# Second layer of a two-layer graph kernel: plain mask matmuls replaced by one Strassen level

## The chip, the cores and the metric

The kernel runs on one core of one Trainium2 chip. The metric is the device time of one execution in microseconds (us). The kernel before takes 930.55 us, the median of 3 runs (930.43 to 931.55). One profiled execution took 931.85 us; its recorded span, from the first to the last recorded instruction, is 929.8 us.

## The reference

There are N = 4096 nodes with 256 features. `adj` is a 4096 x 4096 matrix of zeros and ones. The first layer is a masked softmax over cosine similarities, the second a mean over neighbours followed by three small matrices. Cut to what matters:

```
Wh = x @ W.T;  sim = Wh @ Wh.T / (norms * norms.T + 1e-8)
mask = (adj > 0) | eye
x1 = layernorm(x + softmax(where(mask, sim, -inf)) @ Wh)

deg = sum(adj > 0, axis=1)
agg = (adj > 0) @ x1 / max(deg, 1)
out = relu(concat(x1 @ W_self + b_self, agg @ W_nb + b_nb) @ W_comb + b_comb)
y = layernorm(x1 + out)
```

The change is about the two lines that begin `deg` and `agg`, and about what feeds them and what they feed.

## The kernel before

The nodes are 32 blocks of 128, in 8 groups of four blocks (GB = 4, GW = 512). All work is written out by hand for five instruction queues; semaphores order them, and each engine runs its list strictly in the written order.

**First layer** (about 64 to 632 us). For a in 0..7 and b > a, `pair(a, b)` makes eight 128 x 512 tiles of exponentials: TensorE multiplies the unit vectors (L1027 to L1029, three fp16 products for fp32-like precision) or turns tiles it has (L1093), ScalarE takes exp (L541), VectorE applies the adjacency (L751, L776), ScalarE and VectorE split the tile into an fp16 head and tail (L548, L783), and TensorE adds up the attention (L1099 to L1101). The scores of a tile are issued three tiles ahead of its attention (AHEAD = 3), which is all the lead that VectorE has. ScalarE also writes each mask tile as fp8 ones and zeros, and SP stores it to HBM (`mask_spill`). When the row of groups a is done, VectorE takes it out of PSUM (`attention_out`, L801) and does the layer norm in pieces (`norm_work`: softmax_scale, residual, moments, normalised, split_x1), which are dealt one by one between the tiles of the next row (the list `between`). For the last two groups there is nothing left to deal them between.

**Second layer** (632 to 930 us). For each target group `aggregate` takes the 2 MB mask of the group from HBM into `mgroup` (two slots) and, for each of its four blocks and each of the 32 source blocks, loads the 128 x 128 fp8 mask as weights and streams x1 of the source, as an fp16 head with a column of ones (257 columns, L1199, the ones give the degree) and as an fp16 tail (256 columns, L1200). The first group runs over the source groups 0 to 5, then 6, then 7, so that it can start before x1 of the last groups is there. A finished block is scaled by 1/degree on ScalarE (L607), transposed on TensorE together with x1 of the block (`turn`, L1233 and L1235), split in head and tail (ScalarE L610, VectorE L940), multiplied with the combined weights (`dense`, 12 matmuls, L1245 to L1247), and finished on VectorE (`block_out`: L946, L950, L952, L953; `finish`: L959) with 1/std from GpSimd (L480, L482). `turn` and `dense` of a block are put inside the matmuls of the next block (`spread`), 6 and 18 source blocks after its start:

```
work = [lambda part=part, block=block: part(*block) for block in blocks for part in (turn, dense)]
return {6 + n * (NB - 8) // len(work): piece for n, piece in enumerate(work)}
```

so that ScalarE and VectorE have several us for each step while TensorE goes on. PSUM banks: four for the aggregation, two for `turn`, two for `dense`.

## Time and profile before

| | us |
|---|---|
| median of 3 runs | 930.55 |
| the profiled execution | 931.85 |
| its span | 929.8 |
| TensorE busy (matmuls) | 900.3 |
| VectorE busy | 608.8 |
| ScalarE busy | 412.5 |
| GpSimd busy | 65.2 |
| first matmul of the second layer, from the start | 632.09 |
| matmuls L1199 and L1200, busy together (2048) | 459.0 |

A matmul's busy time is longer than its place in the stream: neighbouring matmuls overlap, and their starts are about 0.11 us apart for 256 columns. So the counts times the distance of the starts give TensorE's time, not the sums of busy time. The span is cut in stretches by the windows view; the granted clock there is a share of TensorE's full 2.4 GHz, and 0.50 is the lower level, 1.2 GHz.

### The profile page before, as it was taken

The page shows a single profiled execution, that of the slowest core. Times are in us where ns is not written, and L with a number is a line of the kernel's source. Part 1 is how long each engine was busy: PE and PEld are TensorE (multiplying, and loading weights), DVE is VectorE, ACT ScalarE, POOL GpSimd, SP SyncE. Part 2 cuts the span into 40 slices and gives each one's busy share as a digit, 9 for nine tenths or more (in the row PEclk, how much of TensorE's full clock was granted, in tenths as well). Part 3 has the DMA queues.
Part 4 walks back from the last instruction along what each step waited for, and adds up shares of the span by engine and source line. Part 5 has one row for each costly group of instructions (what it writes and reads, how often), then busy time and mean ns, then how long its engine had stood idle before and what let it go on. Part 6 is the DMA issues. An engine that isn't in the chain of part 4 may idle for free.

```text
span 929.8 us, 21704 instructions
## 1 busy us (share of the span) xinstructions
PE 900.3 (97%) x7279; PEld 726.2 (78%) x7279; DVE 608.8 (65%) x1286; ACT 412.5 (44%) x701; POOL 65.2 (7%) x175
## 2 busy tenths in 40 slices
PE   7989999999999999999999999989899999999996
PEld 6867777777777777777777777768778888888885
DVE  2787786888766886688778788898543333333333
ACT  4955665666656565656656555550111011111110
POOL 2300000000000000000000000002110000000000
...
GB/s 257 73 150 169 147 147 157 136 171 148 157 148 154 175 153 164 138 192 143 168 178 151 165 255 151 180 117 129 70 130 41 119 125 27 120 124 23 124 28 17
DMA packets 113346, 126.03 MB, mean 136 GB/s; under 512 B 39105, under 2 KB 90594, under 8 KB 112130
## 3 DMA queue, kind: packets, MB, share of 16 engines
...
q8 instruction: 33, 0.54, 0.2%
...
## 4 chain that ended last, share of the span: by engine, by line
issue 87%; PE 5%; POOL 5%; DVE 1%; POOLq 1%; DMA 0%; ACT 0%; SPq 0%; DVEq 0%
PE ps L995 3%; POOL rstd L482 3%; POOL var_eps L480 1%; PE ps L1007 1%; DMA feat_lo<-xT 0%; PE ps L1050 0%; PE ps L1077 0%; POOLq L481 0%; DVE work L640 0%; POOLq L479 0%; DVE work L751 0%; ACT prob_hi L548 0%; DVE big L632 0%; DVE mix_extremes L709 0%; POOLq L484 0%
## 5 line engine op out<-in xcount | busy, mean ns | idle before, releaser
L1099 PE MATMUL ps<-feat_hi,prob_hi 128*128 128x257 f16 (+1 forms) x1024 | 280.0, 273 | 0.5
L1101 PE MATMUL ps<-feat_hi,prob_lo 128*128 128x257 f16 (+1 forms) x1024 | 279.6, 273 | 0.0
L1100 PE MATMUL ps<-feat_lo,prob_hi 128*128 128x256 f16 (+1 forms) x1024 | 278.9, 272 | 0.0
L1199 PE MATMUL ps<-big,mgroup 128*128 128x257 f16 x1024 | 229.5, 274 | 1.9 <-DVE big L839 1.9
L1200 PE MATMUL ps<-big,mgroup 128*128 128x256 f16 x1024 | 229.5, 274 | 0.0
L783 DVE SCALAR_TENSOR_TENSOR prob_lo<-work,prob_hi 128x512 f16<-128x512 f32 x256 | 175.8, 687 | 74.8 <-ACT prob_hi L548 72.3
L548 ACT ACTIVATE prob_hi<-work 128x512 f16<-128x512 f32 x256 | 154.6, 625 | 102.7 <-DVE work L776 48.7
L541 ACT ACTIVATE work<-ps 128x512 f32<-128x512 f32 (+2 forms) x144 | 79.3, 555 | 131.9 <-PE ps L1029 114.4
L553 ACT ACTIVATE mask<-work 128x1024 fp8e4<-128x1024 f32 x128 | 133.5, 1043 | 0.0
L1100 PEld LDWEIGHTS ps<-feat_lo,prob_hi 128*128 128x128 f16 x1024 | 100.3, 98 | 25.2
L1099 PEld LDWEIGHTS ps<-feat_hi,prob_hi 128*128 128x128 f16 x1024 | 100.0, 98 | 25.5 <-DVE prob_lo L783 1.5
L1199 PEld LDWEIGHTS ps<-big,mgroup 128*128 128x128 fp8e4 x1024 | 100.6, 98 | 14.8 <-DVE big L839 2.2
L1027 PE MATMUL ps<-unitT_lo,unitT_hi 128*128 128x512 f16 (+3 forms) x288 | 103.9, 362 | 6.9 <-DVE work L766 2.6
L1200 PEld LDWEIGHTS ps<-big,mgroup 128*128 128x128 fp8e4 x1024 | 100.6, 98 | 11.8
L1101 PEld LDWEIGHTS ps<-feat_hi,prob_lo 128*128 128x128 f16 x1024 | 100.0, 98 | 12.7
L607 ACT ACTIVATE agg_rows<-ps,rdeg 128x256 f32<-128x256 f32 x32 | 15.1, 473 | 212.7 <-DVE rdeg L935 212.7
L1028 PE MATMUL ps<-unitT_hi 128*128 128x512 f16 (+3 forms) x288 | 103.7, 361 | 0.0
L1029 PE MATMUL ps<-unitT_hi,unitT_lo 128*128 128x512 f16 (+3 forms) x288 | 103.7, 361 | 0.0
L751 DVE SCALAR_TENSOR_TENSOR work<-adj_sb,work 128x512 f32<-128x512 int32 x112 | 77.2, 689 | 27.8 <-ACT work L541 25.4
L776 DVE SCALAR_TENSOR_TENSOR work<-adj_sb,ps 128x512 f32<-128x512 int32 x112 | 76.2, 680 | 0.0
L1093 PE MATMUL ps<-ident,work 128*128 128x128 f32 x448 | 67.5, 273 | 1.5 <-DVE work L751 1.4
L480 POOL TENSOR_TENSOR var_eps<-meanvar,ln_eps 128x1 f32<-128x1 f32 x64 | 13.0, 203 | 796.3 <-DVE meanvar L824 552.4
...
## 6 DMA issues: line engine op xcount, KB each, us to landing
adj_sb<-adjT SPq DMA_DIRECT2D x128, 512.0 KB, 3.9
mask_spill<-mask SPq DMA_DIRECT2D x128, 128.0 KB, 2.7
mgroup<-mask_spill SPq DMA_DIRECT2D x8, 2048.0 KB, 8.3
...
```

The costliest lines, as they stand in the source:

```text
L541: act.activation(expo[:, r, first:], score_ps(r)[:, first:], ACT.Exp, scale=1.0 / (UNIT_SCALE * UNIT_SCALE)).then_inc(exp_ready, 1)
L548: act.activation(prob_hi[:, s, :], prob[:, s, :], ACT.Copy, scale=PROB_SCALE).then_inc(prob_hi_ready, 1)
L553: act.activation(mask[:, u_slot, :], prob[:, s:s + 2, :].rearrange("p r i -> p (r i)"), ACT.Sign, saturate=False).then_inc(mask_ready, 1)
L783: dve.scalar_tensor_tensor(out=prob_lo[:, s, :], in0=prob[:, s, :], scalar=PROB_SCALE, in1=prob_hi[:, s, :], op0=ALU.mult, op1=ALU.subtrac ...
L1027: pe.matmul(to, unitT_hi[:, k, src], unitT_lo[:, k, tgt], start=(k == 0), stop=False)
L1028: pe.matmul(to, unitT_hi[:, k, src], unitT_hi[:, k, tgt], start=False, stop=False)
L1029: ins = pe.matmul(to, unitT_lo[:, k, src], unitT_hi[:, k, tgt], start=False, stop=(k == KD - 1))
L1099: pe.matmul(acc(D + 1), prob_hi[:, s, cols], feat_hi[:, jb, 0:D + 1], start=start, stop=False)
L1100: pe.matmul(acc(D), prob_hi[:, s, cols], feat_lo[:, jb, :], start=False, stop=False)
L1101: return pe.matmul(acc(D + 1), prob_lo[:, s, cols], feat_hi[:, jb, 0:D + 1], start=False, stop=stop)
L1199: pe.matmul(agg_ps(q, D + 1), lhsT, x1_hi_of(jb // GB)[:, jb % GB, 0:D + 1], start=(jb == 0), stop=False)
L1200: ins = pe.matmul(agg_ps(q, D), lhsT, x1_lo_of(jb // GB)[:, jb % GB, :], start=False, stop=(jb == NB - 1))
```

## The change

The product mask @ x1 is cut in 2 x 2 pieces three ways: two target groups at a time (a "chunk", four of them), source groups in pairs (p = 0..3, an even and an odd group), and the 256 features in two halves. One Strassen level turns the eight piece products of a chunk and pair into seven.

- **Operands.** Masks no longer are the weights: the weights are 128 x 128 pieces of x1, as fp16 head and tail, and the mask moves, 512 columns at a time (L1474, L1475). A chunk is seven products of 32 matmuls each. Each product needs one mask operand: n11 and n22 (masks negated by the sign bit) and five differences d1, d2, d5, d6, d7. fp8 ones and zeros are bytes, so VectorE makes them by xor, as 16-bit words, 4096 words per partition and operand (`negate`, `difference`), d1 with 32-bit words (`difference_d1`).
- **Sources.** For each pair seven fp16 source pieces, five of them sums or differences of x1 halves: GpSimd adds (`sources`), VectorE splits (`source`) and copies the two plain ones (`plain_sources`). They lie where the unit vectors and features of the first layer were.
- **Degrees.** The ones column is gone. VectorE adds up mask bytes as 16-bit words over the source blocks (`degrees`, nine instructions for a target group) and TensorE sums the partitions (`degree_sums`).
- **Layer norm of x1.** The normalising and the head move from VectorE to GpSimd (`normalised`).
- **Output of a chunk.** The results come transposed, so agg needs no turn: ScalarE copies three of the products out (`keep`), GpSimd and VectorE add them up (`kept_sums`, `sums_12`, `sums_21`, `sum_of`), ScalarE and VectorE split (`agg_head`, `agg_tail`). x1 is stored to HBM as head and tail and comes back turned by DMA (`load_x1T`, four 256 KB transposes ahead of the second layer, two per group after that). `dense` has its self and neighbour part in two halves of one bank, two banks in turn, and `block_out` scales the neighbour part by 1/degree.
- **Masks from HBM** come as four 1 MB pieces per chunk, issued when all products of the chunk before last are done. Those of chunk 0 are loaded after a = 2, and its degrees, negations and d1 stand in `between` of a = 3.

```diff
+QUAD = NB // 2 * GW
+X1_SCALE = 1024.0
+SUM_SCALE = 0.5
+PRODUCTS = (("n11", 0, 0), ("n22", 1, 1), ("d1", 2, 2), ("d5", 3, 6), ("d2", 4, 5), ("d6", 0, 3), ("d7", 2, 4))
+NPROD = len(PRODUCTS)
+OPERAND_COUNT = {"n11": 1, "n22": 2, "d1": 3, "d5": 4, "d7": 5, "d2": 6, "d6": 7}
...
+            def load_raw(c, name):
+                to = unit_of(c, name).rearrange("p (r n) -> p r n", r=NPAIR)
+                ig, odd = {"n11": (2 * c, 0), "d7": (2 * c, 1), "d6": (2 * c + 1, 0), "n22": (2 * c + 1, 1)}[name]
+                sync.dma_start(to, mask_spill[ig].rearrange("p (r two b) i -> p two r (b i)", two=2, b=GB)[:, odd]).then_inc(raw_loaded[name][c % 2], 16)
...
+            def store_x1(a):
+                sync.wait_ge(x1_ready, (a + 1) * GB)
+                wait(sync, x1_stored, 16 * a)
+                wait(sync, x1h_stored, 16 * 2 * a)
+                sync.dma_start(x1_spill[a], x1_rows_of(a)).then_inc(x1_stored, 16)
+                for h, of in enumerate((x1_hi_of(a), x1_lo_of(a))):
+                    sync.dma_start(x1h_dram[h, a].rearrange("(q p) d -> p q d", p=P), of).then_inc(x1h_stored, 16)
...
+            store_x1(G - 2)
+            sync.wait_ge(attn_done, G * NB)
+            load_x1T(0)
+            load_x1T(1)
+            store_x1(G - 1)
+            sync.wait_ge(source_ready, NPAIR * NSRC)
+            sync.wait_ge(x1h_stored, 16 * 2 * G)
+            load_raw(1, "d7")
...
+            for c in range(1, NCHUNK):
+                sync.wait_ge(prod_done, NPROD * c)
+                if c + 1 < NCHUNK:
+                    for name in raw_loaded:
+                        load_raw(c + 1, name)
+                finish(2 * c - 2)
+                finish(2 * c - 1)
...
+            def normalised(a, q):
+                inv_std(a * GB + q, q)
+                if q == 0 and a % 2:
+                    wait(pool, x1_stored, 16 * (a - 1))
+                elif q == 0:
+                    pool.wait_ge(attn_done, tiles_before(a + 1)[0])
+                pool.wait_ge(rstd_ready, a * GB + q + 1)
+                to = x1_rows_of(a)[:, q, :]
+                steps.join(steps.step(pool.tensor_scalar(to, summed[:, q, 0:D], meanvar[:, q, 0:1],
+                                                         rstd[:, q:q + 1], ALU.subtract, ALU.mult)))
+                pool.tensor_scalar(x1_hi_of(a)[:, q, :], to, X1_SCALE, None, ALU.mult).then_inc(rows_hi_ready, 1)
...
+            def degrees(c, group, unit):
+                names = (("n11", "d7"), ("d6", "n22"))[1 - group]
+                total, quarter = words(unit[:, 0:QUAD // 2]), (words(unit[:, QUAD // 2:3 * QUAD // 4]), words(unit[:, 3 * QUAD // 4:]))
+                half, n = QUAD // 4, QUAD // 8
+                for name, part_sum in zip(names, quarter):
+                    dve.wait_ge(raw_loaded[name][c % 2], 16 * (c // 2 + 1))
+                    of = words(unit_of(c, name))
+                    chain.join(chain.step(dve.tensor_tensor(total, of[:, 0:half], of[:, half:], ALU.add)))
+                    chain.join(chain.step(dve.tensor_tensor(part_sum, total[:, 0:n], total[:, n:], ALU.add)))
+                both = words(unit[:, QUAD // 2:])
+                chain.join(chain.step(dve.tensor_scalar(both, both, 3, 0x1F1F, ALU.logical_shift_right, ALU.bitwise_and)))
+                a, b = quarter
+                chain.join(chain.step(dve.tensor_tensor(a, a, b, ALU.add)))
+                chain.join(chain.step(dve.tensor_tensor(a[:, 0:n // 2], a[:, 0:n // 2], a[:, n // 2:], ALU.add)))
+                to = words(degree_bytes[:, group, :])
+                chain.join(chain.step(dve.tensor_tensor(to, a[:, 0:n // 4], a[:, n // 4:n // 2], ALU.add)))
+                wait(dve, degree_done, c)
+                dve.tensor_copy(degree16[:, group, :], degree_bytes[:, group, :]).then_inc(degree16_ready, 1)
+            def negate(c, name, unit):
+                dve.wait_ge(raw_loaded[name][c % 2], 16 * (c // 2 + 1))
+                wait(dve, operand_ready, c * NPROD + OPERAND_COUNT[name] - 1)
+                of = words(unit_of(c, name))
+                chain.join(chain.step(dve.tensor_scalar(words(unit), of, 4, 0x8080, ALU.logical_shift_left, ALU.bitwise_and)))
+                dve.tensor_tensor(of, of, words(unit), ALU.bitwise_xor).then_inc(operand_ready, 1)
+            def difference(c, name, plus, minus):
+                dve.wait_ge(operand_ready, c * NPROD + OPERAND_COUNT[name] - 1)
+                dve.tensor_tensor(words(unit_of(c, name)), words(unit_of(c, plus)), words(unit_of(c, minus)), ALU.bitwise_xor).then_inc(operand_ready, 1)
+            def difference_d1(c):
+                dve.wait_ge(operand_ready, c * NPROD + OPERAND_COUNT["d1"] - 1)
+                dve.scalar_tensor_tensor(out=unit_of(c, "d1").bitcast(U32), in0=unit_of(c, "n11").bitcast(U32),
+                                         scalar=0x7F7F7F7F, in1=unit_of(c, "n22").bitcast(U32), op0=ALU.bitwise_and, op1=ALU.bitwise_xor).then_inc(operand_ready, 1)
+            def first_masks():
+                scratch = part(big_bytes, 0)
+                pieces = [lambda: dve.wait_ge(x1h_stored, 16 * 2 * 2), lambda: degrees(0, 1, scratch), lambda: degrees(0, 0, scratch),
+                          lambda: negate(0, "n11", scratch), lambda: negate(0, "n22", scratch), lambda: difference_d1(0)]
...
+            def sums_12(c):
+                dve.wait_ge(prod_done, c * NPROD + 4)
+                dve.wait_ge(kept_ready, c * 3 + 2)
+                dve.wait_ge(pair_kept, c * 2 + 2)
+                five = prod_ps(PRODUCTS[3][1])
+                dve.tensor_tensor(kept["s3"], five, kept["s3"], ALU.add).then_inc(sum_ready, 1)
+                chain.join(chain.step(dve.scalar_tensor_tensor(out=kept["s2"], in0=five, scalar=-1.0, in1=kept["s2"],
+                                                               op0=ALU.mult, op1=ALU.add)))
+                dve.sem_inc(prod_read, 1)
...
+            def block_out(c, v, q):
+                b, slot = v * GB + q, q % 2
+                group = v % 2
+                wait(dve, y_stored[q], v * 16)
+                chain.join(chain.step(dve.scalar_tensor_tensor(out=rows[:, q, :], in0=dense_ps(slot, 0), scalar=mix_scales[:, 2:3],
+                                                               in1=bias_bc[:, :], op0=ALU.mult, op1=ALU.add)))
+                dve.scalar_tensor_tensor(out=rows[:, q, :], in0=dense_ps(slot, 1), scalar=rdeg[:, c % 2, group * GB + q:group * GB + q + 1],
+                                         in1=rows[:, q, :], op0=ALU.mult, op1=ALU.add).then_inc(dense_read, 1)
...
+            for c in range(NCHUNK):
+                more = c + 1 < NCHUNK
+                inverse_degrees(c)
+                if c:
+                    group_out(c - 1, 2 * c - 2)
+                if more:
+                    degrees(c + 1, 1, scratch_unit)
+                    degrees(c + 1, 0, scratch_unit)
+                    negate(c + 1, "n11", scratch_unit)
+                    negate(c + 1, "n22", scratch_unit)
+                if c:
+                    group_out(c - 1, 2 * c - 1)
+                sums_12(c)
+                agg_tail(c, 0, "s3", 1, 1)
+                if more:
+                    difference_d1(c + 1)
+                    difference(c + 1, "d5", "d7", "n11")
+                    difference(c + 1, "d7", "d7", "n22")
+                sums_21(c)
+                agg_tail(c, 1, "s4", 0, 0)
+                if more:
+                    difference(c + 1, "d2", "d6", "n22")
+                    difference(c + 1, "d6", "d6", "n11")
+                sum_of(c, 5, "s1")
+                agg_tail(c, 2, "s1", 0, 1)
+                sum_of(c, 6, "s2")
+                agg_tail(c, 3, "s2", 1, 0)
+            group_out(NCHUNK - 1, G - 2)
+            group_out(NCHUNK - 1, G - 1)
...
-            def add_neighbours(slot, q, blocks, tails):
-                for jb in blocks:
-                    lhsT = mgroup[:, slot, jb * GW + q * P:jb * GW + (q + 1) * P]
-                    pe.matmul(agg_ps(q, D + 1), lhsT, x1_hi_of(jb // GB)[:, jb % GB, 0:D + 1], start=(jb == 0), stop=False)
-                    ins = pe.matmul(agg_ps(q, D), lhsT, x1_lo_of(jb // GB)[:, jb % GB, :], start=False, stop=(jb == NB - 1))
-                    if jb in tails:
-                        tails[jb]()
-                return ins
...
+            def multiply(c, k, pairs):
+                name, bank, n = PRODUCTS[k]
+                of = unit_of(c, name).bitcast(F8)
+                for p in pairs:
+                    hi, lo = source_of(p, n)
+                    for r in range(GB):
+                        at = slice((p * GB + r) * GW, (p * GB + r + 1) * GW)
+                        pe.matmul(prod_ps(bank), hi[:, r, :], of[:, at], start=(p == 0 and r == 0), stop=False)
+                        ins = pe.matmul(prod_ps(bank), lo[:, r, :], of[:, at], start=False, stop=(p == NPAIR - 1 and r == GB - 1))
+                if pairs[-1] == NPAIR - 1:
+                    ins.then_inc(prod_done, 1)
...
+            for pairs in (range(0, NPAIR - 2), range(NPAIR - 2, NPAIR - 1), range(NPAIR - 1, NPAIR)):
+                for k in range(5):
+                    pe.wait_ge(operand_ready, OPERAND_COUNT[PRODUCTS[k][0]])
+                    if pairs[-1] < NPAIR - 1:
+                        pe.wait_ge(source_ready, (pairs[-1] + 1) * NSRC)
+                    else:
+                        pe.wait_ge(source_ready, pairs[-1] * NSRC + PRODUCTS[k][2] + 1)
+                    if pairs[0] == 0 and k == 4:
+                        pe.wait_ge(attn_copied, NB)
+                    multiply(0, k, pairs)
+                if pairs[0] == 0:
+                    degree_sums(0)
+            product(0, 5)
+            product(0, 6)
+            for c in range(1, NCHUNK):
+                degree_sums(c)
+                dense(c - 1, 2 * c - 2)
+                product(c, 0)
+                dense(c - 1, 2 * c - 1)
+                for k in range(1, NPROD):
+                    product(c, k)
+            dense(NCHUNK - 1, G - 2)
+            dense(NCHUNK - 1, G - 1)
```

**How the lists change.** TensorE, the second layer, from the middle of a block before (one `dense` between aggregation matmuls; "mgroup" is the mask):

```order
L1235 MATMUL ps<-ident,agg_rows 128x128 x2
L1199 MATMUL ps<-big,mgroup 128x257
L1200 MATMUL ps<-big,mgroup 128x256
...
L1245 MATMUL ps<-mixw_hi,damp 128x256 [waits dense_read,tr_lo_ready,tr_ready]
L1246 MATMUL ps<-mixw_lo,damp 128x256
L1247 MATMUL ps<-mixw_hi,damp 128x256
```

TensorE now, the start of chunk 1 (degree sums, `dense` of group 0, product n11, `dense` of group 1, product n22), only the first row of each block or product:

```order
L1504 MATMUL ps<-ones,w0T_sb 128x1 [waits rdeg_ready,degree16_ready]
...
L1521 MATMUL ps<-mixw_hi,mask 128x256 [waits agg_lo_ready]
...
L1474 MATMUL ps<-mgroup,unitT_hi 128x512 [waits sum_ready,operand_ready]
...
L1521 MATMUL ps<-mixw_hi,prob_lo 128x256 [waits dense_read,x1T_loaded1]
...
L1521 MATMUL ps<-mixw_hi,summed 128x256 [waits agg_lo_ready]
...
L1521 MATMUL ps<-mixw_hi,prob_lo 128x256 [waits dense_read]
...
L1474 MATMUL ps<-mgroup,unitT_hi 128x512 [waits kept_ready,operand_ready]
```

The `dense` of four blocks now stand together, each behind a `dense_read` that VectorE gives two blocks earlier, and six of the seven products stand behind the second four.

VectorE before, one block of the second layer (`damp` is the tail of the turned block):

```order
L932 TENSOR_SCALAR deg<-ps 128x1 [waits agg_ready]
L935 RECIPROCAL rdeg<-deg 128x1 [waits deg_step]
L957 REGISTER_ALU
L54 REGISTER_ALU [waits rstd_ready]
L959 TENSOR_SCALAR rows<-summed,meanvar,rstd 128x256 [waits y_stored0]
L940 SCALAR_TENSOR_TENSOR damp<-ps,damp 128x512 [waits tr_ready]
L946 SCALAR_TENSOR_TENSOR summed<-ps,mix_scales,bias_bc 128x256 [waits dense_done]
```

VectorE now, in chunk 1, what stands between the last output block of group 0 and the first of group 1 (the masks of chunk 2: two degree sums, two negations):

```order
L1202 SCALAR_TENSOR_TENSOR rows<-ps,mix_scales,bias_bc 128x256 [waits dense_done]
...
L1029 TENSOR_TENSOR work<-mgroup 128x2048 [waits raw_loaded_n11_0]
...
L1029 TENSOR_TENSOR work<-mgroup 128x2048 [waits raw_loaded_d7_0,dve_step]
...
L1029 TENSOR_TENSOR work<-mgroup 128x2048 [waits raw_loaded_d6_0]
...
L1046 TENSOR_SCALAR work<-mgroup 128x4096 [waits operand_ready,raw_loaded_n11_0]
...
L1046 TENSOR_SCALAR work<-mgroup 128x4096 [waits operand_ready,raw_loaded_n22_0]
...
L1202 SCALAR_TENSOR_TENSOR rows<-ps,mix_scales,bias_bc 128x256 [waits y_stored0,dense_done]
```

The output blocks of group 1, and with them the `dense_read` of its first block, stand behind 22 mask instructions.

VectorE now, in the first layer at a = 3, three neighbouring tiles (L928 and L935 are the mask and tail of a tile) with the degrees of chunk 0 between them:

```order
L935 SCALAR_TENSOR_TENSOR prob_lo<-work,prob_hi 128x512 [waits prob_ready,prob_hi_ready]
L1029 TENSOR_TENSOR big<-mgroup 128x2048 [waits raw_loaded_n11_0]
...
L928 SCALAR_TENSOR_TENSOR work<-adj_sb,ps 128x512 [waits prob_hi_ready,mask_ready,adj_loaded3,score_done]
...
L1029 TENSOR_TENSOR big<-mgroup 128x2048 [waits raw_loaded_d6_0]
...
L1046 TENSOR_SCALAR big<-mgroup 128x4096 [waits raw_loaded_n11_0]
L1047 TENSOR_TENSOR mgroup<-mgroup,big 128x4096 [waits dve_step]
```

Where before a layer norm piece of one or two instructions stood after each tile, nine mask instructions now stand after each of two tiles, and a negation after the third.

## Rows read from the trace of the kernel before

**Rows 1.** Windows: stretch and length, busy us per engine, granted clock, DMA share, GB/s.
```profile
300.00:400.00 100.00, 99.48 (x777) 76.28 (x775) 76.29 (x151) 60.59 (x93) 2.92 (x8) 1.00 0.56 159
590.00:630.00 40.00, 35.69 (x280) 26.29 (x279) 36.46 (x82) 21.02 (x34) 3.34 (x8) 1.00 0.46 137
700.00:800.00 100.00, 99.20 (x903) 88.48 (x902) 33.95 (x94) 12.84 (x24) 8.76 (x24) 1.00 0.27 94
```
**Rows 2.** Timeline of TensorE: start, us, line. Starts of 512 and 256 columns; second layer.
```profile
299.65 0.38 PE L1028 MATMUL ps<-unitT_hi 128*128 128x512 f16 x1
...
300.73 0.27 PE L1099 MATMUL ps<-feat_hi,prob_hi 128*128 128x257 f16 x1
...
301.83 0.27 PE L1100 MATMUL ps<-feat_lo,prob_hi 128*128 128x256 f16 x1
...
632.09 0.27 PE L1199 MATMUL ps<-big,mgroup 128*128 128x257 f16 x1
...
919.65 0.27 PE L1200 MATMUL ps<-big,mgroup 128*128 128x256 f16 x1
```
**Rows 3.** Timeline of VectorE at the end of the first layer.
```profile
630.09 1.22 DVE L808 TENSOR_TENSOR summed<-summed,big 128x1028 f32<-128x1028 f32 x1
...
642.68 1.65 DVE L801 SCALAR_TENSOR_TENSOR summed<-feat_hi,diag_w,ps 128x257 f32<-128x257 f16 x4
...
658.25 0.42 DVE L839 SCALAR_TENSOR_TENSOR big<-rows,big 128x256 f16<-128x256 f32 x1
```
**Rows 4.** Groups by line and shape: busy us, mean ns, idle before and its releaser.
```profile
L808 DVE TENSOR_TENSOR summed<-summed,big 128x1028 f32<-128x1028 f32 x7 | 8.6, 1223 | 0.0
...
L794 DVE TENSOR_TENSOR big<-big,ps 128x257 f32<-128x257 f32 x64 | 23.6, 410 | 0.0
...
L647 DVE COPY unitT_lo<-ps 128x1024 f16<-128x1024 f16 x8 | 5.5, 682 | 0.0
...
L683 DVE TENSOR_SCALAR feat_hi<-big,scales 128x1024 f16<-128x1024 f32 x3 | 2.3, 751 | 0.0
...
L783 DVE SCALAR_TENSOR_TENSOR prob_lo<-work,prob_hi 128x512 f16<-128x512 f32 x256 | 175.8, 687 | 74.8 <-ACT prob_hi L548 72.3
...
L610 ACT ACTIVATE damp<-ps 128x512 f16<-128x512 f32 x32 | 19.1, 597 | 45.2 <-PE ps L1235 45.2
```
**Rows 5.** Groups by line: the parts of one output block.
```profile
L946 DVE SCALAR_TENSOR_TENSOR summed<-ps,mix_scales,bias_bc 128x256 f32<-128x256 f32 x32 | 15.5, 484 | 76.9 <-PE ps L1247 76.9
...
L952 DVE BATCH_NORM_STATS2 stats<-summed 128x6 f32<-128x256 f32 x32 | 13.7, 427 | 1.1
...
L950 DVE SCALAR_TENSOR_TENSOR summed<-summed,xres 128x256 f32<-128x256 f32 x32 | 13.6, 426 | 1.8
...
L959 DVE TENSOR_SCALAR rows<-summed,meanvar,rstd 128x256 f32<-128x256 f32 x32 | 13.2, 414 | 6.1 <-POOL rstd L482 5.5
...
L953 DVE BATCH_NORM_AGGREGATE meanvar<-stats 128x2 f32<-128x6 f32 x32 | 5.8, 182 | 4.4 <-DVE stats L952 4.3
```
**Rows 6.** Windows of 2 us around a wait of TensorE for x1 of group 7.
```profile
656.00:658.00 2.00, 0.81 (x8) 0.47 (x5) 1.86 (x7) 0.00 (x0) 0.88 (x2) 1.00 0.00 0
658.00:660.00 2.00, 1.26 (x8) 0.97 (x9) 0.64 (x2) 0.00 (x0) 0.00 (x0) 0.76 0.24 96
660.00:662.00 2.00, 2.00 (x11) 1.43 (x10) 0.32 (x2) 0.47 (x1) 0.00 (x0) 0.50 0.41 166
662.00:664.00 2.00, 2.00 (x18) 1.67 (x17) 0.64 (x4) 0.00 (x0) 0.00 (x0) 0.88 0.59 191
```
**Rows 7.** Timeline of GpSimd: the same instruction beside busy and beside idle VectorE.
```profile
634.01 0.80 POOL L482 TENSOR_TENSOR rstd<-var_eps,minus_half 128x1 f32<-128x1 f32 x1
...
919.20 0.54 POOL L482 TENSOR_TENSOR rstd<-var_eps,minus_half 128x1 f32<-128x1 f32 x1
```
**Rows 8.** DMA issues: count, KB each, median us to landing.
```profile
mgroup<-mask_spill SPq DMA_DIRECT2D x8, 2048.0 KB, 8.3
```

502 lines of the change are left out of this document (290 added, 212 removed).

## The prediction

> **What bounds the kernel now.** I read the windows view first. In mid first layer TensorE is busy 99.5 of 100 us and VectorE 76; in the second layer 99.2 and 34 [rows 1]. TensorE is the bound; VectorE has slack on average. The exception is the last row group of the first layer, 590 to 630: VectorE 36.5 of 40 and TensorE 35.7 [rows 1]. Second, TensorE's timeline for what a matmul takes in the stream: five 512-column ones in 300.73 - 299.65 = 1.08 us, so 0.2165 us each, and ten 256-column ones in 1.10 us, so 0.11 us each; the second layer starts at 632.09 and its last aggregation at 919.65 [rows 2]. Third, VectorE at that border: the sums of group 6 begin at 630.1, attention_out of group 7 at 642.7, the last tail of x1 is at 658.25 [rows 3]. Fourth, prices. A 32-bit two-source sum takes 410 ns for 257 elements and 1223 for 1028, so 0.14 us + 1.05 ns per element: one per cycle. A 16-bit COPY of 1024 out of PSUM takes 682 ns, two per cycle, and TENSOR_SCALAR f32 to f16 of 1024 751 ns [rows 4].
>
> **What goes and what comes on TensorE.** Before, the aggregation is 2048 x 0.11 = 225 us. After, a product is 32 x 0.2165 = 6.93 us, a chunk of seven 48.5, four chunks 194: 31 us less. The turns of `turn` go too: the span 632.09 to 919.65 is 287.6, less 225 and less 31 blocks of `dense` at 12 x 0.11 = 1.32, so 22 us [rows 2]. Degree sums are 32 matmuls of one column, about 1 us. If nothing waited, TensorE would be through the products and six of the eight groups of `dense` after 194 + 24 x 1.32 + 1 = 227 us, at 859. The question is what waits.
>
> **Price of the mask work.** No row shows a 16-bit two-source operation on SBUF. Bounds: one per cycle as the f32 sums do (2048 words 2.30 us, 4096 words 4.45), or two per cycle as the 16-bit COPY does (1.22 and 2.30) [rows 4]. I take two: the operand width is what sets those two rows apart. For TENSOR_SCALAR on 16-bit words in and out, two per cycle is the upper bound, four the lower: the f32 one in SBUF already runs two per cycle, and 16-bit data doubles the copies [rows 4]. I take four (4096 in 1.22, 2048 in 0.68). So `degrees` of one target group: 2 x 1.22 + 3 x 0.68 + 0.68 + 0.41 + 0.27 + 0.41 = 6.3, and 6.7 with the joins between. A `negate`: 1.22 + 2.30 + join = 3.55. A difference 2.3. Of a chunk, 2 x 6.7 + 2 x 3.55 = 20.5 us stand in one piece between two output groups; 6.9 and 4.6 more between sums.
>
> The Trainium skill (VectorE: DVE Perf Modes, section The perf-mode tier table) caps tensor_tensor at 2x for 16-bit and lets tensor_scalar go to 4x; by it the sum is the one I make. Had the width of the COPY row come from its being single-source, it would be the rival below.
>
> **Chunk 0.** TensorE starts at 632.1 as before. Products n11, n22, d1, d5 on pairs 0 and 1 are 64 matmuls, 13.9 us, to 646. Then d2 needs its difference, which stands behind five pieces of the last norm_work, after attention_out of group 7 at 642.7 [rows 3] (4 x 0.41) and 2.3 us for itself and the mixed norm pieces: about 651.8. Stall 5.9 us. The rest follows VectorE's sources of pair 3 closely and ends near 687.4 (632.1 + 48.5 + 5.9 + 0.9).
> VectorE meanwhile: norm pieces of group 7 and d6 to 661, five sources of pair 3 at 0.3 + 0.69 each, GpSimd's sums ahead of them, and copies, to 670. It then does `inverse_degrees` and the masks of chunk 1, whose d7 is only loaded when the sources are ready (1 MB; 2 MB take 8.3 us to land [rows 8], so about 676). 1.9 of the 20.5 us are done by then: 676 + 18.6 = 694.6. Only then come, in the written order, seven sums and tails of chunk 0 at about 0.7 each (512 elements at one per cycle [rows 4]), 11.5 us of differences between them, and 1.9 for joins: the third tail, for which `dense` of group 0 waits, is there at 712.9. TensorE, after the degree sums, waits from 688.4: **24.5 us**.
>
> **Chunks 1 and 2**, each counted from A, when the third tail is there. `dense` of four blocks: its blocks come at VectorE's rate, because each needs the `dense_read` of two before. One output block is 0.48 (twice, as there are now two parts) + 0.43 + 0.43 + 0.18 + joins = 2.25, finish 0.45 with its wait: 2.7 us per block [rows 5]. TensorE is at A + 8.5 after four, does n11 to A + 15.4 and blocks 4 and 5 to A + 18. Block 6 needs `dense_read` of block 4. VectorE gives it at A + 2.8 (its start) + 11.8 (a group: four blocks and the last finish) + 20.5 (masks) + 1.0 (both parts of block 4) = A + 36.1. **Stall 18 us.** Then blocks 6 and 7 at VectorE's pace, 3.5, and six products, 41.6: 81.2 us per chunk. Chunk 3 has no mask work behind it, so block 6 waits only for the cadence: 20.7 + 41.6 = 62.3. After the last product come the last sum and tail, 1.5, and two output groups at VectorE's pace, 2 x 11.8: 25.1. The store and the end are 2.2.
>
> Sum: 632.1 + 56.3 (chunk 0 and degree sums) + 24.5 + 81.2 + 81.2 + 62.3 + 25.1 + 2.2 = **965**.
>
> **Clock.** When TensorE had waited some 2 us for x1 of group 7 (656 to 658: 0.81 busy), its granted clock fell from 1.00 to 0.76, 0.50 (its lower level, 1.2 GHz) and 0.88 over the next 6 us, though it was busy again [rows 6]: 0.48 + 1.0 + 0.24 = 1.7 us lost. There are now four waits of 6 to 25 us, longer than that one: 2 each, +8. Bounds 0 (the matmuls behind them wait for VectorE anyway) and 3.4 each, twice the row.
>
> **First layer.** Three things are put where VectorE has three tiles (about 6.7 us) of lead. At a = 3 the 22 mask instructions and d1, 22.8 us, follow three neighbouring tiles. The lead pays 6.7 of them, and VectorE's idle 24% over these 29.5 us pays 7.1: +9. The 4 MB at a = 2 compete with loads and mask stores at 0.56 DMA share [rows 1]: +3 (0 to 8). In the last groups VectorE, already 91% busy [rows 1], loses four normalisings and four heads per group but gains, per pair of groups, five sources of 1 us and four copies of 0.4, some 5 us net: +3. Sum +15, bounds 0 (the leads absorb all, as the pieces are few) and 30.
> Normalising goes to GpSimd, which no row prices at this size. Lower bound 0.4 (VectorE's row), upper 2.0; at 1 it is hidden, at 2 the waits of the tails add a few us more. GpSimd's pow took 0.80 us beside busy VectorE and 0.54 beside idle [rows 7], so the two share something. The Trainium skill (SBUF - State Buffer, section SBUF: two separate sides) calls it an exclusive lock of one port pair; rows 7 agree in sign, and by that rule the f32 sources on GpSimd (512 elements) stretch both engines, which would use up the upper half of my 30 us.
>
> Total 965 + 8 + 15 = 988 for the span. The profiled run's time is 2.05 above its span (931.85 against 929.8) and 1.3 above the median, so **989 us**, 6.3% more than before.
>
> **Rivals.**
> 1. 16-bit two-source operations run one per cycle. Mask work between the output groups: four of 2048 words (+1.08 each), six of 1024 (+0.54), 0.4 twice for the short ones, two of 4096 (+2.15) = +13; four differences +8.6, of which 5 on the path. Three places (the start of chunks 1, 2 and 3) at 18, and +7 at a = 3: **+61, 1050**. For: no row shows the mode. Against: width decides in the two rows there are.
> 2. The four 256 KB transposing transfers ahead of the second layer stand on SP before `store_x1(7)` and the reload of x1. If one takes 5 us or more, `x1_stored` comes 20 us late, and VectorE stands before its whole second layer for it: +20, **1009**. Or the first layer loses its upper bound of 30 us instead of 15: **1004**. For: group 7's tail is the last thing of the layer; against: the 2 MB load lands in 8.3 us [rows 8].
> 3. The other side, faster: the mask work is hidden and TensorE's saved work decides. 632.1 + 227 + 5.9 (d2) + 25.1 + 2.2 = 892, with 2 for the clock, 5 for the first layer and 0.75: **900**. It decides from the point where what stands between the output groups is at most 18 - 15.6 = 2.4 us instead of 20.5; to break even, 58 us must go of 24.5 + 18 + 18 + 8 + 15. For it: in the second layer VectorE is busy 34 of 100 us [rows 1], so on average there is room. Against it: the lists are strict, and what counts is the order in which VectorE comes to a thing, not its average.
> 4. Milder waits: no first-layer loss, clock free, mask work a third cheaper (every 16-bit operation at four per cycle): 965 - 3 x 7 = 944, **935 to 960**.
>
> **Numbers.** A difference within 0.2% is about what a measurement of this kernel cannot tell from no change. The forecast's own case (965 to 1010) has 60%; rival 1 14%; rival 2 12%; rival 4 6%; rival 3 6%; an end within 0.2% of before, between rivals 3 and 4, 2%. So faster 0.06, same 0.02, slower 0.92. The range 958 to 1050 leaves out rival 3, most of rival 4 and the worst of rival 1 (four per cycle untrue as well: +90).
>
> **What would show it.** TensorE idle about 24 us before the first L1521 with VectorE's L1167 as releaser, and about 19 us twice before the third block of the second `dense`, released by L1204. L1029 at 1.2 us (2.3 is rival 1), L1047 at 2.3 (4.5). Granted clock 0.50 in the windows right behind these waits. The first product of the second layer starts between 632 and 662. Wrong if the second `dense` runs without a wait, or if the first layer ends later than 662.

## The result

| | us |
|---|---|
| before, median of 4 runs | 930.91 |
| after, median of 4 runs (1020.71 to 1024.41) | 1023.58 |
| ratio, 95% interval | 1.0984 (1.0968 to 1.1001) |
| the profiled execution of after, its span | 1023.38, 1021.6 |
| forecast, range | 989, 958 to 1050 |

The kernel became slower, as forecast, but by 93 us and not by 58. The time lies inside the forecast's range, but outside its own case of 965 to 1010. The second layer starts at 680.65 instead of 632.09 and takes 341 us (1021.6 - 680.65). The forecast had 341 for it (965 - 632.1 and 8 for the clock) and 15 for the first layer, which lost 48.6. Net, the whole miss lies in the first layer. One of the four executions of e4_xres_first below took 1341.92 us at a mean granted clock of 0.65, and its ratio is made from the other three.

### The profile page after: what moved, and what is told of

The parts are those of the page before. It is cut to its first block, busy times and chain, and to the rows that moved or that the text cites. A ratio compares the mean times of both kernels' runs of the same rounds, so it can differ in the third digit from the quotient of the medians.

```text
span 1021.6 us, 18791 instructions
## 1 busy us (share of the span) xinstructions
PE 877.5 (86%) x6031; PEld 604.8 (59%) x6031; DVE 757.5 (74%) x1374; ACT 395.9 (39%) x665; POOL 190.2 (19%) x267
## 4 chain that ended last, share of the span: by engine, by line
PE 58%; DVE 22%; issue 7%; DMA 4%; POOL 4%; ACT 3%; SPq 1%; DVEq 0%; ACTq 0%; POOLq 0%
PE ps L1370 7%; PE ps L1371 7%; PE ps L1372 7%; PE ps L1474 6%; PE ps L1475 6%; PE ps L1298 4%; PE ps L1300 4%; PE ps L1299 4%; PE ps L1364 4%; DMA xres<-x 3%; PE ps L1266 3%; DVE prob_lo L935 2%; ACT mask L701 2%; DVE work L928 2%; DVE work L1029 1%
## 5 line engine op out<-in xcount | busy, mean ns | idle before, releaser
L1370 PE MATMUL ps<-feat,prob_hi 128*128 128x257 f16 (+1 forms) x1024 | 282.7, 276 | 2.2 <-DVE prob_lo L935 1.7
L1372 PE MATMUL ps<-feat,prob_lo 128*128 128x257 f16 (+1 forms) x1024 | 281.7, 275 | 0.0
L1371 PE MATMUL ps<-feat,prob_hi 128*128 128x256 f16 (+1 forms) x1024 | 281.3, 275 | 0.0
L935 DVE SCALAR_TENSOR_TENSOR prob_lo<-work,prob_hi 128x512 f16<-128x512 f32 x256 | 182.2, 712 | 69.2 <-ACT prob_hi L696 66.2
L1298 PE MATMUL ps<-unitT_lo,unitT_hi 128*128 128x512 f16 (+3 forms) x288 | 106.1, 370 | 39.8 <-DVE work L928 21.4
L1370 PEld LDWEIGHTS ps<-feat,prob_hi 128*128 128x128 f16 x1024 | 101.0, 99 | 30.2 <-issue 5.1
L1371 PEld LDWEIGHTS ps<-feat,prob_hi 128*128 128x128 f16 x1024 | 101.3, 99 | 26.5 <-issue 1.5
L1372 PEld LDWEIGHTS ps<-feat,prob_lo 128*128 128x128 f16 x1024 | 100.9, 99 | 13.7
L753 ACT ACTIVATE feat<-ps 128x512 f32<-128x512 f32 x12 | 7.2, 597 | 183.7 <-PE ps L1475 183.7
L928 DVE SCALAR_TENSOR_TENSOR work<-adj_sb,ps 128x512 f32<-128x512 int32 x112 | 76.2, 681 | 0.0
L1474 PE MATMUL ps<-big,feat 128*128 128x512 fp8e4 x160 | 61.7, 386 | 12.3 <-DVE big L1052 11.1
L1298 PEld LDWEIGHTS ps<-unitT_lo,unitT_hi 128*128 (+1 forms) x288 | 28.6, 99 | 64.5 <-DVE work L918 15.2
L1475 PE MATMUL ps<-big,feat 128*128 128x512 fp8e4 x160 | 61.7, 385 | 0.0
L1364 PEld LDWEIGHTS ps<-ident,work 128*128 128x128 f32 x448 | 51.9, 141 | 6.3 <-issue 3.7
```

Source lines behind the costliest of these rows:

```text
L935: dve.scalar_tensor_tensor(out=prob_lo[:, s, :], in0=prob[:, s, :], scalar=PROB_SCALE, in1=prob_hi[:, s, :], op0=ALU.mult, op1=ALU.subtrac ...
L1298: pe.matmul(to, unitT_hi[:, k, src], unitT_lo[:, k, tgt], start=(k == 0), stop=False)
L1364: ins = pe.transpose(score_ps(j)[:, (2 * s + u) * P:(2 * s + u + 1) * P], expo[:, 2 * h + u, (2 * qp + s) * P:(2 * qp + s + 1) * P], ident ...
L1370: pe.matmul(acc(D + 1), prob_hi[:, s, cols], feat_hi_of(g)[:, r, 0:D + 1], start=start, stop=False)
L1371: pe.matmul(acc(D), prob_hi[:, s, cols], feat_lo_of(g)[:, r, :], start=False, stop=False)
L1372: return pe.matmul(acc(D + 1), prob_lo[:, s, cols], feat_hi_of(g)[:, r, 0:D + 1], start=False, stop=stop)
```

## The profile after

Windows of after (stretch and length, busy us per engine, granted clock, DMA share, GB/s), against [rows 1]:

```profile
300.00:400.00 100.00, 96.07 (x747) 72.99 (x745) 78.65 (x150) 57.30 (x89) 20.04 (x21) 1.00 0.56 159
...
450.00:500.00 50.00, 39.78 (x274) 27.98 (x275) 43.27 (x65) 21.58 (x33) 0.00 (x0) 0.90 0.36 101
...
750.00:800.00 50.00, 16.71 (x98) 10.53 (x98) 45.89 (x64) 3.12 (x5) 3.27 (x8) 0.71 0.35 116
800.00:850.00 50.00, 42.91 (x201) 20.78 (x202) 30.85 (x41) 3.08 (x5) 5.77 (x10) 0.88 0.14 32
```

From 750 to 800 TensorE is busy a third of the time and VectorE nine tenths: the bound has changed sides. Who waited for whom, TensorE (line waited for: us in total, times, longest):

```profile
PE ps L1521 <- DVE rows L1204: 44.2, 13, 17.4
PE ps L1521 <- DVE mask L1167: 23.1, 1, 23.1
PE ps L1298 <- DVE work L928: 21.4, 13, 5.4
PE ps L1298 <- DVE work L918: 12.8, 10, 3.6
PE ps L1474 <- DVE big L1052: 11.1, 1, 11.1
...
PE ps L1298 <- DVE work L914: 4.9, 2, 4.1
```

The first two are the second layer's: once 23.1 us before `dense` for the third tail (L1167), and inside the 44.2 the two waits of 17.4 us for `dense_read` (L1204). The three lines with L1298, 39 us, are the first layer's. Of the second layer, where these waits stand (TensorE's timeline, idle time before in brackets):

```profile
680.65 0.38 PE L1474 MATMUL ps<-mgroup,unitT_hi 128*128 128x512 fp8e4 x1
...
705.70 0.61 PE L1474 MATMUL ps<-big,feat 128*128 128x512 fp8e4 x1 [11.07 <-DVE big L1052]
...
772.89 0.40 PE L1521 MATMUL ps<-mixw_hi,mask 128*128 128x256 f16 x1 [23.11 <-DVE mask L1167]
...
807.09 0.40 PE L1521 MATMUL ps<-mixw_hi,prob_lo 128*128 128x256 f16 x1 [17.43 <-DVE rows L1204]
...
888.00 0.40 PE L1521 MATMUL ps<-mixw_hi,prob_lo 128*128 128x256 f16 x1 [17.43 <-DVE rows L1204]
```

A chunk is 888.00 - 807.09 = 80.9 us. VectorE's groups (busy us, mean ns, idle before), which answer to the bounds taken from [rows 4] and [rows 5]:

```profile
L1204 DVE SCALAR_TENSOR_TENSOR rows<-ps,rdeg,rows 128x256 f32<-128x256 f32 x32 | 15.5, 484 | 1.1
...
L1052 DVE TENSOR_TENSOR mgroup<-mgroup 128x4096 uint16<-128x4096 uint16 x4 | 9.1, 2281 | 0.1
...
L1046 DVE TENSOR_SCALAR work<-adj_sb 128x4096 uint16<-128x4096 uint16 x4 | 4.9, 1223 | 0.2
L1029 DVE TENSOR_TENSOR big<-mgroup 128x2048 uint16<-128x2048 uint16 x4 | 4.9, 1222 | 0.1
```

With two sources a 16-bit word costs (2281 - 1222) / 2048 = 0.52 ns, half of the 1.05 ns that the prediction read off the f32 sums. With one source, 4096 words take no longer than 2048 words do with two.

**Where the first layer lost its time.** The start of `attention_out` on VectorE (L801 before, L953 after) marks the end of each row a. How much longer than before each kernel takes for each row, in us, read from its one profiled execution; the last column is the start of the second layer. The other kernels are the experiments below. e7_second_layer, whose first layer is that of after, starts its second layer at 682.8, so a difference of 2 us in the last column says little.

| | to a = 1 | a = 2 | a = 3 | a = 4 | a = 5 | a = 6 | then | second layer |
|---|---|---|---|---|---|---|---|---|
| after | -1.2 | 4.4 | 19.0 | 4.3 | 6.5 | 13.0 | 2.6 | 680.65 (+48.6) |
| e2_spread | -1.5 | 4.4 | 11.9 | 6.0 | 4.5 | 13.4 | 2.7 | 673.5 |
| e3_norm_vector | -1.9 | 5.0 | 20.8 | 10.7 | 8.9 | 10.8 | 1.4 | 687.8 |
| e4_xres_first | -1.8 | 2.8 | 18.1 | 3.0 | 2.6 | 9.9 | 2.8 | 669.5 |
| e5_no_sources | 0.5 | 1.8 | 18.8 | 1.8 | 7.4 | 8.5 | 1.6 | 672.5 |
| e6_no_masks | -1.6 | 4.4 | 5.1 | 4.7 | 4.5 | 12.0 | 2.3 | 663.5 |
| e8_all | -0.3 | 2.8 | 4.7 | 4.7 | 3.0 | 9.6 | 1.4 | 658.0 |

## The experiments

**e1_out_first.** One edit in VectorE's list of the second layer:

```diff
                 if c:
                     group_out(c - 1, 2 * c - 2)
+                if c:
+                    group_out(c - 1, 2 * c - 1)
                 if more:
                     degrees(c + 1, 1, scratch_unit)
...
                     negate(c + 1, "n22", scratch_unit)
-                if c:
-                    group_out(c - 1, 2 * c - 1)
```

> The changed kernel with one edit on VectorE: in chunks 1 and 2 the second output group comes ahead of the degrees and negations of the next chunk. Theory (the 17.4 us waits of TensorE before the third block of the second dense come from the order of VectorE's list): both waits go, each chunk falls from 80.9 us to about 65, where VectorE's own work per chunk (23.6 output, 20.5 masks, 11.5 differences, 9 sums and tails) becomes the bound: 32 us less, about 992 us. Rival (VectorE's total work sets the pace already, the wait only moves to the next chunk): at most 10 us less, 1014 us or more.

Measured 992.7 us (990.99 to 993.56), ratio 1.0676 (1.0655 to 1.0698): 31 us less than after, where the theory had 32. TensorE's timeline around the second and third chunk:

```profile
773.03 0.40 PE L1521 MATMUL ps<-mixw_hi,mask 128*128 128x256 f16 x1 [23.19 <-DVE mask L1167]
...
791.62 0.28 PE L1521 MATMUL ps<-mixw_hi,prob_lo 128*128 128x256 f16 x1 [0.52 <-DVE rows L1204]
...
838.62 0.28 PE L1521 MATMUL ps<-mixw_hi,mask 128*128 128x256 f16 x1 [3.22 <-DVE mask L1167]
```

The 17.4 us waits are gone; a chunk is 838.62 - 773.03 = 65.6 us, and the 3.22 us wait for the third tail is new. VectorE is busy for 57.7 of these 65.6 us (windows view, 773.03 to 838.62), not for the 65 of the expectation, and its list still reaches the third tail after TensorE does. So the order cost 15.3 us per chunk (80.9 - 65.6), and the new wait of 3.2 is about what is left of the 17.4.

**e2_spread and e6_no_masks.** The first deals the mask work of chunk 0 out over row 3, one or two instructions between tiles. The second leaves most of that work out: it makes the degree sums and negations of chunk 0 on 16 words, d1 stays whole, and its output is not the reference's. An excerpt of each edit:

```diff
-                pieces = [lambda: dve.wait_ge(x1h_stored, 16 * 2 * 2), lambda: degrees(0, 1, scratch), lambda: degrees(0, 0, scratch),
-                          lambda: negate(0, "n11", scratch), lambda: negate(0, "n22", scratch), lambda: difference_d1(0)]
-                return pieces
...
+                pieces = []
+                for group in (1, 0):
+                    for name, to in zip(names[group], (a, b)):
+                        pieces += [lambda name=name: halve(name, name == "n11"), lambda to=to: quarter(to)]
+                    pieces += [shift, lambda group=group: last(group)]
```
```diff
-                    chain.join(chain.step(dve.tensor_tensor(total, of[:, 0:half], of[:, half:], ALU.add)))
...
+                    w = 16 if c == 0 else half
+                    chain.join(chain.step(dve.tensor_tensor(total[:, 0:w], of[:, 0:w], of[:, half:half + w], ALU.add)))
```

> The changed kernel with the mask work of chunk 0 dealt out in the row a = 3 as 17 pieces of one or two instructions instead of five pieces of up to nine (and VectorE's loop over the pairs of that row unrolled to have places for them). The same work. Theory (clumping: VectorE's lead of three tiles is used up at once, TensorE waits 5.4, 4.3 and 1.3 us and its clock falls): row a = 3, now 19 us longer than in the kernel before, loses most of that: 13 to 17 us less, about 1009 us. Rival (the work itself does not fit: 22.8 us against 24% idle of an 80 us row, which norm pieces need too): 5 us less or no change, 1018 to 1024.

> The changed kernel with the degree sums and negations of chunk 0 in row 3 made on 16 words instead of 256 to 4096 (d1 stays whole): it leaves out 20 of the 22.8 us, and its output is not the reference's. It is the other end of the experiment that only dealt them out, which gained 7 us. Theory (7 us of row 3's 19 were the clump, the rest is volume): row 3 is 1 to 3 us longer than in the kernel before, 16 to 18 us less in all, about 1006 us. Rival (what was left after the dealing out is the 4 MB load or GpSimd's work in that row): 7 to 10 us less, 1014 us or more.

Measured: e2 1016.6 us (1.0947, 1.0922 to 1.0973), 7 us less; e6 1006.9 us (1.0824, 1.0801 to 1.0846), 17 less. Row 3 (table): 19.0, then 11.9 dealt out, 5.1 without. The theory of clumping held for 7 us only; 7 more are volume, and 5.1 stay even without the work (e6 had expected 1 to 3), d1's 2.3 among them. The windows show why. One line of each: all of row 3 in before (400 to 480), then the stretch with the mask work in after, and in e2:

```profile
400.00:480.00 80.00, 79.48 (x622) 60.86 (x620) 63.33 (x127) 47.86 (x74) 2.92 (x8) 1.00 0.57 161
```
```profile
446.00:466.00 20.00, 10.35 (x53) 5.77 (x52) 19.42 (x27) 4.63 (x7) 0.00 (x0) 0.77 0.26 71
```
```profile
450.00:495.00 45.00, 39.10 (x288) 27.32 (x287) 42.67 (x65) 22.73 (x34) 0.00 (x0) 1.00 0.41 118
```

In after TensorE gets only half of 20 us, at a granted clock of 0.77. Dealt out, the clock stays at 1.00, but VectorE is 95% busy for 45 us: 63 us of old work and 23 of new do not fit into 80. Length of a row and VectorE's busy time in it (windows view), in us:

| | row 3: length | VectorE busy | row 6: length | VectorE busy |
|---|---|---|---|---|
| before | 80.3 | 63.4 | 32.5 | 29.8 |
| after | 99.4 | 82.7 | 45.5 | 36.7 |
| e2_spread | 92.3 | 81.8 | | |
| e6_no_masks | 85.4 | 67.3 | | |
| e5_no_sources | | | 40.9 | 31.1 |

Against e6, e2 has 14.5 us more work on VectorE in row 3 and the row is about 7 us longer: dealt out, half of the work is paid. In one heap (after) 15.4 us of work cost 13.9.

**e3_norm_vector.** Normalising and head back on VectorE:

```diff
+            def x1_rows(a, q):
+                ...
+                chain.join(chain.step(dve.tensor_scalar(x1_rows_of(a)[:, q, :], summed[:, q, 0:D], meanvar[:, q, 0:1],
+                                                        rstd[:, q:q + 1], ALU.subtract, ALU.mult)))
...
+                dve.tensor_scalar(x1_hi_of(a)[:, q, :], x1_rows_of(a)[:, q, :], X1_SCALE, None, ALU.mult).then_inc(rows_hi_ready, 1)
```

> The changed kernel with the normalising and the fp16 head of x1 back on VectorE; GpSimd keeps 1/std and the sums of the sources. Theory (a chain of 2.6 us on GpSimd behind each block's moments, for which VectorE waits some 8 us at each of groups 6 and 7, where nothing else is left to do): about 10 us less at the end of the first layer, a few given back in rows 4 to 6 where VectorE gets 2.8 us more per group: 1013 to 1017 us. Rival A (GpSimd's work beside VectorE's slows all tiles: the tail of a tile takes 712 ns against 687 before): 20 us or more less, 1003 or under, with 687 ns again. Rival B (VectorE's total is the bound of the late rows): slower, 1026 or more.

Measured 1021.8 us (1.1001, 1.0974 to 1.1028), 2 us less, no difference that these runs settle. The sum hides two effects of opposite sign, one as rival B had it and one as the theory had it: rows 4 and 5 lose 6.4 and 2.4 us more, with more work on VectorE there, and in the profiled execution (1019.5 us) the second layer falls from 341 to 330 us. The wait that goes is this one of after, 15.7 us of it behind 680:

```profile
DVE big L980 <- POOL big L600: 22.1, 14, 3.0
```

Rival A fell as to its size: a tail of a tile took 710 ns on average, as in after, though GpSimd normalised nothing. What does stretch the tails, e5 shows.

**e4_xres_first.** In SyncE's list, the load of x goes ahead of the stores of x1:

```diff
-                if 0 < a < G - 1:
-                    store_x1(a - 1)
                 wait(sync, summed_ready, a * GB)
                 sync.dma_start(xres[:, :, :], x_v[a]).then_inc(xres_loaded, 16)
+                if 0 < a < G - 1:
+                    store_x1(a - 1)
```

> The changed kernel with SyncE's load of x for the residual ahead of the three stores of x1 of the group before. Theory (VectorE idles 12 us in all for that load at the start of rows, and TensorE's waits of 2.3, 1.0, 2.1 and 3.6 us follow it): the waits on the load go, 4 to 8 us less, about 1018. Rival (VectorE's idle time there is covered by the lead of three tiles): no change, 1022 to 1025.

Measured 1012.5 us (1.0886, 1.0862 to 1.0911): 11 us less, more than expected, and all of it in the first layer (669.5 against 680.65). VectorE's waits in after, and then in e4:

```profile
DVE summed L970 <- DMA xres<-x: 12.1, 6, 3.9
```
```profile
DVE summed L970 <- DMA xres<-x: 1.1, 2, 0.8
```

Six waits of up to 3.9 us stand in the first 10 us of the rows. Around the start of row 3 the load of x is issued at 404.74 in after, behind the three stores and 1.6 us into the row, and in e4 at 400.74, as the row starts. Of the 12.1 us 11.0 go, and TensorE's second layer starts 11.1 us earlier: one for one.

**e5_no_sources.**

```diff
+                few = slice(0, 4 if p < NPAIR - 1 and n < 4 else P)
+                hi, lo, term = hi[:, :, few], lo[:, :, few], term[:, :, few]
```

> The changed kernel with four of the five summed sources of pairs 0, 1 and 2 made on 4 columns per block instead of 128, on GpSimd and on VectorE: this leaves out some 6 us of VectorE's and 5.5 us of GpSimd's work in each of the rows 2, 4 and 6 of the first layer, and its output is not the reference's. Theory (VectorE has no room left in the late rows, so its added volume comes out one for one in row 6 and in part in rows 2 and 4): second layer starts 9 to 13 us earlier, 1011 to 1015 us. Rival (only clumps cost, and sources stand alone between tiles): 4 us or less, 1019 to 1023.

This kernel leaves out most of four of the five summed sources of pairs 0 to 2, and its output is not the reference's. Measured 1009.7 us (1.0838, 1.0819 to 1.0858), 14 us less. The profiled execution is the slowest of the four, 1014.84 us, 8.5 less than after's, and by the table its first layer gives 8.2 of them, a little under the 9 to 13 of the theory; the other 5 us of the median no trace shows. Rows 2, 4 and 6, those that hold a pair's sources, gain 2.6, 2.5 and 4.5 us, for 4.8, 4.9 and 5.6 us less work on VectorE: half in the early rows, four fifths in row 6.

The run also settles what stretches the tails of the tiles. Their group in after and in e5:

```profile
L935 DVE SCALAR_TENSOR_TENSOR prob_lo<-work,prob_hi 128x512 f16<-128x512 f32 x256 | 182.2, 712 | 69.2 <-ACT prob_hi L696 66.2
```
```profile
L936 DVE SCALAR_TENSOR_TENSOR prob_lo<-work,prob_hi 128x512 f16<-128x512 f32 x256 | 177.0, 692 | 71.6 <-ACT prob_hi L697 68.7
```

The mean is 687 ns in before, 712 in after, and 692 without most of GpSimd's sums. In after 16 of the 256 tails take over 725 ns: seven stand beside GpSimd's sums (L612), up to 1766 ns, and cost 4.6 us together, nine beside its normalising and heads, 1.6 us.

**e7_second_layer.** The second layer's lists written anew, with a shorter negation and masks loaded one by one as their buffers come free; the first layer as it was. TensorE, and the new negation on VectorE:

```diff
                 degree_sums(c)
-                dense(c - 1, 2 * c - 2)
                 product(c, 0)
-                dense(c - 1, 2 * c - 1)
-                for k in range(1, NPROD):
-                    product(c, k)
+                product(c, 1)
+                for n in range(3):
+                    dense(c - 1, 2 * n, 2 * n + 2)
+                    product(c, n + 2)
+                dense(c - 1, 6, 8)
+                product(c, 5)
...
+                dve.tensor_scalar(of, of, 23.0 / 7.0, 0.25, ALU.mult, ALU.add).then_inc(operand_ready, 1)
```

(A mask byte is 0 or 0x38, and 0x38 x 23/7 is 0xB8, the same number with its sign bit, in either byte of a word.)

> The changed kernel with the second layer's lists rewritten and its first layer as it was. TensorE: the first two products of a chunk ahead of any dense, then two blocks of dense behind each product. VectorE: the output blocks in pairs with mask work between, chunk 0's sums ahead of chunk 1's masks, a negation as one multiplication by 23/7 on 16-bit words (1.2 us instead of 3.5). SyncE loads masks as single buffers come free. The last product is cut in two, with the first blocks of dense between. Theory (all that the second layer lost were orders): chunk 0 ends at 746, then TensorE's own 60 to 61 us per chunk, and an end 19 us behind the last product: 680.7 + 65 + 183 + 21 = 950, 951 us. Rival (VectorE's 59 us of work per chunk and its waits make the pace, 66 us): 966 us or more.

Measured 962.0 us (1.032, 1.0297 to 1.0343): 62 us less than after, 11 more than the theory's 951. The waits of 17 and 23 us are gone, the one of 11 us for d2 stays, and one of 10 us is new, on the degree sums of chunk 1, which I had left ahead of its products:

```profile
761.20 0.38 PE L1571 MATMUL ps<-ones,w0T_sb 128*128 128x1 f16 x8 [10.13 <-DVE w0T_sb L1246]
```

**e8_all.** That second layer, e4's order, e2's dealing out (over rows 3 and 4, with the short negation), and groups 6 and 7 normalised on VectorE.

> The second layer as in the rewritten lists, with the first layer mended too: the load of x for the residual first, chunk 0's masks dealt out over rows 3 and 4 (with the short negation), groups 6 and 7 normalised on VectorE, the others on GpSimd. Theory (the effects add: 11 for the load, 10 to 12 for the masks, 6 to 9 for the last groups): 951 - 29 = 922 us, 915 to 930. Rival (they overlap, as each only gives VectorE back the same idle time): 935 us or more.

Measured 931.5 us (1.0001, 0.9987 to 1.0016): no change against before. Against e7 it is 30.5 us less (961.96 to 931.48), so the 29 of the theory came, and the miss of its 922 is what e7 already had above 951. By the profiled executions the first layer gave 24.8 us of it (682.8 to 658.0), and the second layer 10.8 (280.3 to 269.5); these two executions lie 35.6 us apart, more than the medians. The 10 us wait of e7 came along. In row 6, with its twelve tiles and the sources of pair 2, 9.6 us stay.

**e9_tuned.** From e8's trace: VectorE is busy for 71.6 of the 78 us from 640 to 718, and GpSimd and VectorE take turns there. GpSimd (first fence) and VectorE (second) of e8:

```profile
673.86 0.34 POOL L588 TENSOR_TENSOR var_eps<-meanvar,ln_eps 128x1 f32<-128x1 f32 x1 [6.42 <-DVE meanvar L982]
...
675.43 2.14 POOL L588 TENSOR_TENSOR var_eps<-meanvar,ln_eps 128x1 f32<-128x1 f32 x1 [0.35 <-DVE meanvar L982]
```
```profile
675.27 2.26 DVE L1075 TENSOR_TENSOR big<-mgroup 128x4096 uint16<-128x4096 uint16 x1
```

The same one-element addition takes 0.34 us, or 2.14 when it starts behind a 16-bit two-source operation of VectorE, and it ends with that one (675.27 + 2.26 = 677.53, 675.43 + 2.14 = 677.57). One of the edits of e9 gives ScalarE the last step of an output block:

```diff
+                    act.activation(rows[:, q, :], rows[:, q, :], ACT.Identity, bias=minus_mean[:, q:q + 1],
+                                   scale=rstd[:, q:q + 1]).then_inc(y_ready, 1)
```

> The kernel with the mended first layer and the rewritten second, and further: ScalarE, idle in the second layer, takes the last step of each output block (with -mean/std from GpSimd) and the fp16 heads of groups 6 and 7 and of the last pair's sources; that pair's sums are made on VectorE, since GpSimd's and VectorE's two-source operations only took turns there (a head took 1.48 us and tails 1.64 us beside a GpSimd sum against 0.41 and 0.69 alone); the difference d2 is used only after the other four products have done pair 2; the differences of a chunk are made in that chunk, its degree sums stand behind its first two products. Theory (VectorE is the bound from the end of the first layer to chunk 2; it loses 8 us at the border and 8 us per chunk): 931.5 - 8 - 2 x 5 = 912 us, 906 to 918. Rival (ScalarE's steps in one list with the copies of products make new waits, or the clock and GpSimd's extra small operations beside VectorE take it back): 922 us or more.

Measured 913.4 us (911.2 to 915.73), where the theory had 912. The ratio to before is 0.9821 (0.9797 to 0.9845): 1.6 to 2.0% less time than before. What each of the edits brings was not run on its own, so it is not shown how much of the 18 us below e8 comes from ScalarE's help, from the sums taken off GpSimd or from the new orders. Windows of its second layer:

```profile
660.00:700.00 40.00, 38.24 (x185) 17.31 (x184) 36.39 (x73) 8.04 (x16) 14.38 (x18) 1.00 0.79 236
700.00:800.00 100.00, 100.00 (x549) 52.38 (x548) 89.17 (x135) 14.78 (x25) 30.12 (x48) 1.00 0.37 113
800.00:890.00 90.00, 90.00 (x513) 49.42 (x512) 65.90 (x118) 14.04 (x24) 29.10 (x61) 1.00 0.26 63
```

TensorE is the bound again, at a granted clock of 1.00. The second layer is 909.4 - 658.65 = 251 us against 298 before: 47 us gained, of which the first layer, 26.6 us longer than before, takes more than half back.

## Why the prediction was right, and where it failed

- **VectorE's prices: right.** 1222 ns for 2048 words, 2281 to 2293 for 4096, 1223 for the 4096-word TENSOR_SCALAR (1.22, 2.30, 1.22 forecast). This settled rival 1. The Trainium skill (VectorE: DVE Perf Modes, section The perf-mode tier table) caps tensor_tensor on 16-bit data in SBUF at 2x and tensor_scalar at 4x. The trace agrees, with the prices above.
- **The wait inside chunks 1 and 2: right,** place, releaser and size: 17.43 us twice against 18, the chunk 80.9 against 81.2. e1 shows its cause by taking it away.
- **The wait before the first dense: right,** 23.1 against 24.5, with L1167 as releaser.
- **d2: place right, size wrong.** 11.07 us against 5.9, and 4.9 (3.7 and 1.2) against 0.9 for pair 3's sources. GpSimd's normalising took 3.35 us (L598) beside the difference d2, not the 1 us I took. From the start of the layer to the third tail it is 772.89 - 680.65 = 92.2 us against 80.8. After that it is 248.7 us against the 260 of 252 and 8 for the clock. These two errors cancel; that the layer came out at 341 is in part luck.
- **The clock: right in kind, and its 8 us were not needed on top.** Behind the wait before 807.09 it shows 0.50 for 4 us and 0.83 for 2:

```profile
807.00:809.00 2.00, 1.92 (x10) 1.36 (x11) 1.86 (x6) 0.00 (x0) 0.68 (x2) 0.50 0.00 0
809.00:811.00 2.00, 2.00 (x11) 1.44 (x10) 1.86 (x7) 0.00 (x0) 0.70 (x3) 0.50 0.02 4
811.00:813.00 2.00, 2.00 (x12) 1.19 (x11) 1.90 (x6) 0.00 (x0) 0.47 (x2) 0.83 0.47 120
```

  That is 2.3 us by the forecast's own way of counting, which had 2. It did cost time: `dense` of the two blocks behind the wait took 4.85 us (807.09 to 811.94) where 3.5 were forecast. Yet chunks 1 and 2 together, from dense to dense, took 162.1 us (772.89 to 934.99) with the clock inside, where the forecast had 162.4 without it, and from there to the end it was 86.6 us against 89.6. The other terms were a little too long.

- **The step that failed is "First layer", +15 with bounds 0 to 30; it was +48.6.** The prediction named as a sign of being wrong that the first layer "ends later than 662"; the second layer starts at 680.65. Four terms were mis-sized or missing. The masks at a = 3: 9 forecast, 14 of the row's 19 shown by e6. Of 22.8 us of work 6.7 were to be paid by the lead and 7.1 by VectorE's idle 24%. Against e6, after has 15.4 us more work on VectorE in that row and is 13.9 longer, so together they paid about 1.5. The load of x, missing: 11 us (e4). The change put two more stores ahead of it on SyncE, and the forecast has no term for what stands behind them. Rows 4 to 6, 3 forecast: 23.8, of which e4 takes 8.3 and e5 6.1, shares that partly overlap. And GpSimd, taken as hidden at 1 us for a normalising, took 1.23 us at the least and mostly 1.6: at groups 6 and 7 VectorE waits for its heads (22.1 us in all, 15.7 of them after 680; with VectorE doing it, e3's second layer is 11 us shorter).
- **The bound was too narrow for a reason:** each added piece was weighed against VectorE's mean idle share. How much of an added piece is paid depends on where it stands: half for the sources in rows 2 and 4 and for masks dealt out over row 3, four fifths in row 6, where VectorE was 92% busy before, and nine tenths in one heap.
- **That the total lies inside the range is in part luck.** The upper end of 1050 was drawn for rival 1, 16-bit operations at half the speed, and that did not happen. The forecast's own case ended at 1010, and no rival had the first layer above 30 us; rival 1's room took up the 34 us that the first layer lost beyond its 15.
- **Rival 2** did not come true by its own mechanism: the turning transfers land in a median of 3.8 and 3.9 us, and no engine waited for them. Its second half, a first layer that loses 30 us and an end at 1004, did in kind, but the loss was 48.6 us.

What stays open: if their effects add up, which no run tests, e4, e6 (with e2 inside it) and e5 explain 11 + 17 + 8 of the 48.6 us, and e3 shows another 3 at the end of the first layer for a normalising on VectorE (2.2 in row 6, 1.2 behind it). About 9 us, mostly of rows 4 to 6, were not split further.
